# A transformer layer on one core: the attention groups written out in halves after a table of places, zero rows filled by transfers, four chunks projected in front, and the tail taken apart

## The reference

```python
x = x + attn(layernorm(x))            # x: 2 x 1024 x 128, f32; 16 heads of width 8
x = x + moe(layernorm(x))             # 2048 tokens
# attn: q, k, v = x@W + b; rotary; att = (q@k.T + bias_of_distance[head]) / sqrt(8), causal,
#       softmax, @ v, then @ Wp + bp
# moe:  probs = softmax(x@Wr); top 2 of 8 experts; position of a token in its expert = running count;
#       512 places for each expert; expert: rms norm, gelu(h@Wg)*(h@Wu) @ Wd + row (128 -> 256 -> 128);
#       out = x + sum of weight*expert row; a token that found no place takes a small shared network (width 64)
```

## Time and profile before

| | us |
|---|---|
| median of 3 runs (lowest to highest) | 473.14 (470.46 to 474.53) |
| the profiled execution, whole | 469.73 |
| its span in the trace | 468.0 |
| PE busy | 383.5 |
| DVE busy | 320.2 |
| POOL busy | 277.1 |
| ACT busy | 212.4 |

### The profile page before, as it was taken

How to read it: one execution, slowest core, us unless ns; L and a number is a source line. 1 busy time by engine, 2 the same in 40 slices (tenths; PEclk the granted TensorE clock), 3 DMA queues, 4 the chain that set the end, 5 groups by cost and what they waited for, 6 DMA issues and landing times.

```text
span 468.0 us, 8283 instructions
## 1 busy us (share of the span) xinstructions
PE 383.5 (82%) x2440; PEld 184.4 (39%) x2440; DVE 320.2 (68%) x702; ACT 212.4 (45%) x471; POOL 277.1 (59%) x229
## 2 busy tenths in 40 slices
PE   3497398699999999997999999985976494999910
PEld 0154143343444434433444444342434151566510
DVE  3989379687786786865867868759566770366614
ACT  1024212377676776764767767755442100233200
POOL 6637800096767857865768668575457383066760
PEclk9999679799999999999999999998897597899975
DMA  7296880650532883507107100062001011123118
GB/s 232 36 275 136 180 191 15 167 97 2 101 74 92 261 183 68 111 5 125 50 4 134 39 4 1 1 201 70 2 30 56 26 45 63 48 91 92 46 45 269
DMA packets 32560, 42.90 MB, mean 92 GB/s; under 512 B 6043, under 2 KB 26395, under 8 KB 31147
## 3 DMA queue, kind: packets, MB, share of 16 engines
q1 hardware_dynamic: 29334, 35.62, 32.5%
q0 software_dynamic: 2048, 4.11, 2.6%
q10 hardware_dynamic: 1136, 2.65, 1.6%
HBM read 27.61 MB, written 12.75 MB: 86 GB/s over the span
## 4 chain that ended last, share of the span: by engine, by line
PE 63%; DVE 15%; DMA 7%; issue 6%; POOL 5%; SPq 1%; ACT 1%; ACTq 0%; DVEq 0%; POOLq 0%
PE ps_av L923 15%; PE ps_st L899 14%; PE ps_slot L827 13%; PE ps_slot L831 5%; PE ps_st L1018 3%; PE ps_slot L1028 3%; POOL slots L609 3%; DVE neg_max L1182 2%; DMA b_grp<-b_all 2%; PE ps_st L1020 2%; PE ps_slot L942 1%; PE ps_av L1020 1%; DMA bcol<-in_L_attn_bk_dram 1%; PE ps_slot L866 1%; POOL parts L618 1%
## 5 line engine op out<-in xcount | busy, mean ns | idle before, releaser
L1182 DVE TENSOR_REDUCE neg_max<-ps_slot 128x1 f32<-128x640 f32 (+7 forms) x184 | 175.9, 990 | 46.4 <-PE ps_slot L831 45.2
L689 ACT ACTIVATE probs<-ps_st 128x512 f32<-128x512 f32 (+3 forms) x384 | 164.6, 494 | 86.4 <-PE ps_st L899 83.5
L594 POOL TENSOR_TENSOR probs<-probs,f_grp 128x960 f32<-128x960 f32 (+2 forms) x70 | 133.8, 1916 | 5.2
L827 PE MATMUL ps_slot<-k_stack,q_stack 128*128 128x512 bf16 (+3 forms) x384 | 102.7, 335 | 9.4 <-DMA b_grp<-b_all 3.4
L899 PE MATMUL ps_st<-q_stack,k_stack 128*128 128x512 bf16 (+3 forms) x384 | 99.8, 332 | 4.3 <-DMA q_stack<-max_rows 2.7
L590 POOL TENSOR_SCALAR_AFFINE_SELECT probs<-probs 128x512 f32<-128x512 f32 x63 | 40.2, 638 | 102.3 <-ACT probs L689 102.3
L923 PE MATMUL ps_av<-probs,v_grp 128*32 128x512 f32 (+3 forms) x768 | 82.3, 502 | 0.6 <-POOL probs L594 0.3
L831 PE MATMUL ps_slot<-b_grp,flip_b 128*128 128x240 bf16 (+2 forms) x288 | 67.6, 259 | 0.0
L899 PEld LDWEIGHTS ps_st<-q_stack,k_stack 128*128 128x128 bf16 x384 | 34.8, 98 | 65.8 <-ACT probs L689 45.8
L827 PEld LDWEIGHTS ps_slot<-k_stack,q_stack 128*128 128x128 bf16 x384 | 36.3, 100 | 47.4 <-DVE neg_max L1182 14.5
L618 POOL DMA_INDIRECT parts<-probs,e_tok x32 | 31.5, 985 | 31.0 <-DVE probs L1434 22.2
(11 more groups left out here) (156 smaller groups left out, 392.2 us busy)
## 6 DMA issues: line engine op xcount, KB each, us to landing
q_stack<-q_parts SPq DMA_DIRECT2D x24, 192.0 KB
f_grp<-f_all SPq DMA_DIRECT2D x6, 512.0 KB, 10.2
slots<-in_c_rows_dram SPq DMA_DIRECT2D x4, 528.0 KB, 6.1
probs<-slots SPq DMA_DIRECT2D x8, 264.0 KB, 2.7
f_all<-g_vec SPq DMA_DIRECT2D x1, 2048.0 KB, 11.3
k_stack<-k_parts SPq DMA_DIRECT2D x16, 128.0 KB
b_grp<-b_all SPq DMA_DIRECT2D x8, 256.0 KB
...
```

What stands on the lines that cost most here:

```text
L594: pool.tensor_tensor(pr, pr, f_grp[:, fbuf, :, fo:fo + hi - lo], ALU.mult).then_inc(near_done, 1)
L689: act.activation(probs[:, u % PBUF, g, c0:512], ps_st[:, n % 3, c0:512], ACT.Exp, scale=SCALE).then_inc(exp_done, 1)
L827: pe.matmul(ps_slot[:, slot, o + lo:o + hi], q_stack[:, buf, g, t * P:(t + 1) * P], k_stack[:, buf, g, lo:hi], start=True, stop=(nlo >= nhi))
L1182: dve.tensor_reduce(neg_max[:, heads[0]:heads[-1] + 1, t], src, AX.X, ALU.max, negate=True).then_inc(slot_used, 1)
```

## The change

The loop is gone: `attention_plan` builds one list (`PLAN`) for the whole of prologue, attention and tokens, and every engine walks it. Eight groups of 48 rows (one ST each) are numbered 0 to 383, and `S_BEFORE`, `M_BEFORE`, `EXTRAS` and `DISPATCH_AT` say ahead of which row or behind which unit each piece stands.

- q and k stacks are stored and loaded by halves of 512 tokens. Group 0's halves go out and in first; its S starts with the first half; M comes twice for each group (`NM` = 2), and ST of query half 0 waits for the first alone.
- S of group 0 stands partly ahead of row 0 (13 units) and partly within its own ST; S of group 1 at rows 16 to 50, later groups about one group ahead.
- No memsets: rows 72 to 79 (8 partitions) and 80 to 127 (48 partitions) are filled by transfers out of a row of zeros (`clear_rows`, on ACT's queue: buffer 0 at the start, buffers 1 and 2 in `LOAD`; and a first one on SP's). `LOAD`, also on ACT, brings the bias tiles of the twelve later heads. The small weights are loaded from POOL's queue.
- `v_all` holds values at a pitch of 9 with the column of ones; AV reads 9 columns from it, and the zero padding and the copy on ACT go. `f_grp` and `b_grp` go too: bias tiles are read from `f_all` and `b_all`.
- All 16 tiles are normed in one go on DVE; chunks 1 to 3 are normalised on ACT. All four chunks are projected in front; the split and the storing of chunks 2 and 3 stand within group 0's ST, and so do six of eight FLIP.
- Batch 0's tokens are worked in groups 3 to 5, with its Newton steps on POOL and its rows on ACT, and its 16 dispatches on POOL in groups 6 and 7. Batch 1 is two spans of four tiles: the first is dispatched while the last is being worked. A and C go through `ps_st` and ACT. F and G stand behind everything, and the scaling of their weights with them.
- Warm-up matmuls are 128 columns wide: 48 and 24 in front, 10 and 6 in the tail, 8 before the experts (before: 8, 8 and 32 of 512 columns).

```diff
-VW = 32
+MAX_ROWS, CLEAR = 3, 80
+VW = D + 1
-STACK_IN = 10 * 16
-PART_OUT = 4 * 16
+STACK_IN = 9 * 16
+HALF_IN = 8 * 16
+NM = 2
+MT = TPB // NM
+PART_OUT, REST_OUT = 8 * 16, 6 * 16
-WARM_FIRST, WARM_STACK, WARM_SLOTS = 8, 8, 32
+WARM_FIRST, WARM_PROJ, WARM_SLOTS = 48, 24, 8
...
+M_AT = (6, 22)
+S_BEFORE = [
+    [0, 0, 0, 0, 0, 0, 0, 0, 0, 0, 0, 0, 0, 2, 4, 5, 6, 7, 7, 10, 11, 12, 13],
+    [16, 16, 16, 16, 16, 17, 18, 20, 23, 24, 24, 27, 28, 28, 31, 35, 35, 36, 38, 41, 43, 47, 50],
+    [52, 56, 56, 58, 59, 63, 66, 68, 72, 72, 75, 76, 76, 79, 79, 82, 82, 84, 86, 89, 91, 95, 98],
...
+M_BEFORE = [(0, 16), (21, 54), (71, 102), (119, 150), (167, 198), (214, 245), (262, 300), (310, 342)]
+DISPATCH_AT = [73, 75, 77, 79, 81, 83, 84, 85, 86, 87, 88, 89, 90, 91, 92, 93]
...
-SPANS = [(0, TPB), (TPB, TT)]
+SPANS = [(0, TPB), (TPB, TPB + CH), (TPB + CH, TT)]
+LAST_NEAR = [2, 3, 5, 7, 9, 10, 11]
...
+LAST = [("DISP", j // 2, j % 2) for j in range(len(DISPATCH_AT), 2 * TPB)] \
+    + [("C", 2), ("AV", NG - 1, NU - 3), ("RI", 1), ("D", 1), ("AV", NG - 1, NU - 2)] + choose(1) \
+    + [("AV", NG - 1, NU - 1), ("EVAC", NG - 1, 1), ("Y", NG - 1, 1), ("PR", 1)] + place(1) \
+    + [("A", 3), ("B", 3), ("WARM", 10), ("BN", 3, 0), ("BN", 3, 1)] + [("RS", 2, j) for j in range(4)] \
+    + [("U", t) for t in range(TT - CH, TT)] + [("RI", 2), ("C", 3), ("D", 2), ("WARM", 6)] + choose(2) + [("PR", 2)] + place(2)
...
+        def clear_rows(eng, first, n, done):
+            for st, rows in ((q_stack, (M_ROW, CLEAR)), (q_stack, (CLEAR, P)), (k_stack, (CLEAR, P))):
+                eng.dma_start(st[rows[0]:rows[1], first:first + n, :, :, :].rearrange("p a h b c -> p (a h b c)").bitcast(F32),
+                              bass.AP(tensor=c_ones.tensor, offset=MAX_ROWS * NBUF * HG * T // 2,
+                                      ap=[[0, rows[1] - rows[0]], [1, n * HG * T // 2]])).then_inc(done, 16)
...
+            for c in range(2):
+                store_part(c, 0, (0,), first_out[0])
+                store_part(c, 1, (0,), first_out[1])
+                sp.wait_ge(first_out[0], 16 * (c + 1))
+                load_q(0, 0, (c,), half_in[c])
+                sp.wait_ge(first_out[1], 16 * (c + 1))
+                load_k(0, 0, (c,), half_in[c])
+            store_parts(0, (1, 2, 3), parts_out[0])
+            store_parts(1, (1, 2, 3), parts_out[1])
+            put_max(0, 0)
+            for c in range(2):
+                sp.wait_ge(parts_out[c], REST_OUT)
+            sp.wait_ge(zero_in[1], 48)
+            load_stack(1)
+            put_max(0, 1)
+            load_stack(2)
+            for n in range(1, NG):
+                put_max(n, 0)
...
+                elif kind == "LOAD":
+                    act.wait_ge(vec_out, 32)
+                    act.wait_ge(half_in[1], HALF_IN)
+                    load_tiles(act, b_all, r_vec, HG, H - HG, toep_rest)
+                    load_tiles(act, f_all, g_vec, HG, H - HG, factors_rest)
+                    clear_rows(act, 1, 2, zero_in[1])
...
+                    if g == 0 and (qb, kt) in ((0, 0), (1, 0)):
+                        pe.wait_ge(mrows_in[qb], 16 * MAX_PARTS * (n + 1))
...
                     for g in range(HG):
-                            mm = pe.matmul(ps_av[32 * g:32 * g + VW, c0:512], v_grp[:, vb, kt, g, :],
+                        mm = pe.matmul(ps_av[32 * g:32 * g + VW, c0:512], v_all[:, n, kt, g, :],
...
+                    elif su == 0:
+                        pe.wait_ge(stack_in[n % NBUF], STACK_IN * fill_of(n))
+                        if n == 1:
+                            pe.wait_ge(zero_in[1], 48)
+                            pe.wait_ge(toep_rest, 16)
...
+            def first_roots(piece):
+                v, t, dst = newton[:, 0:2, 0:TPB], newton[:, 2:4, 0:TPB], rstd[:, :, 0:TPB]
+                if piece == 1:
+                    pool.wait_ge(guess_done, 1)
+                after(pool.tensor_tensor(t, dst, dst, ALU.mult))
+                after(pool.tensor_tensor(t, t, v, ALU.mult))
+                after(pool.tensor_scalar(t, t, -0.5, 1.5, ALU.mult, ALU.add))
+                after(pool.tensor_tensor(dst, dst, t, ALU.mult))
```

More of the change, by code:

```diff
@@ new lines, in score_items @@
+def score_items():
+    out, late = [], []
+    for n in range(NG):
+        for su in range(len(SUNITS)):
+            out.append((S_BEFORE[n][su], ("S", n, su)))
+            late = [(left - 1, m) for left, m in late]
+            if su in M_AT:
+                late.append((M_LATE if n else 0, ("M", n, M_AT.index(su))))
+            while late and late[0][0] <= 0:
+                m = late.pop(0)[1]
+                out.append((M_BEFORE[m[1]][m[2]], m))
+    return out + [(M_BEFORE[m[1]][m[2]], m) for _, m in late]
@@ L483, in _, with stack_rows @@
[L483 to L492 removed]
+            load_tiles(sp, b_all, r_vec, 0, HG, toep_in)
+            load_tiles(sp, f_all, g_vec, 0, HG, factors_in)
+            def stack_rows(stack, buf, row, n, halves):
+                return stack[row:row + n, buf, halves[0]:halves[-1] + 1, :, :].rearrange("p h g t -> p h (g t)")
@@ L976, in _ @@
+            for what in FALLBACK:
                 kind, c = what
```

1396 lines of the change are left out of this document (743 added, 653 removed), and 13 rows, old and new, of tables (EXTRAS, S_BEFORE).

## The result

The changed kernel takes 479.0 us (median of 4 runs, 477.6 to 480.7), the kernel before 472.7 in the same comparison: ratio 1.0137, 95% interval 1.008 to 1.019. It is slower by a little over 1%, clear of noise, where the forecast was 434 and faster. The profiled execution has a span of 476.5. The page's totals say little: PE is busy for 10 us more than before, and the low stretches of its clock, in slices 6 to 8 and behind the attention, are still there, at other places.

The account below looks back on a forecast made before the run. PE was taken to bound the loop's steps, leaving gains around them. Stages of 43 + 58.5 + 191.4 + 26 + 41.5 + 70.6 gave a 431.0 us span, 432.7 whole, forecast 434; range 422 to 451.

Parts of the forecast that it names:

- Vectors, turn and the first projection are as before: Front: these pieces keep their earlier times, so the first rotation starts near 19.5 us instead of 27.3.
- The pace of the chunks: Front: a chunk costs DVE 5.4 us, four chunks 22; then two FLIP, and S starts at 43.
- 1.9 to land, more under load: First S to group 1: landing time of the first half's maxima rows, putting them in q at 53 to 55 us.
- Rival 1: Zeroing and LOAD are late, put_max(0,1) queues behind load_stack(1), row 16 starts at 82 to 84: +11, 445 us; chance 0.17.
- The rate I took, 260 GB/s: First S to group 1: rate seen in the trace, held against rival 1's front mean of 172 GB/s for 5.1 MB.
- Six steps of 30.5 are 183.2: Groups 1 to 6: base time at the old loop's step, before token work, savings and waits bring it to 191.4.
- AV's saving: Groups 1 to 6: nine instead of 32 columns take 0.02 us off each of 96 units, 2 in all.
- rival 4: AV's nine-column matmuls are not run side by side: +225 us, about 650, so slower; chance 0.04.
- Rival 2: The middle groups stretch: each of seven groups takes 3 us more than forecast, 453 us; chance 0.12.
- The distance over 33: Groups: the forecast fails if like points lie over 33 us apart; 30.5 to 32 was expected for groups 1 to 6.
- ST of group 7: Last ST group: ACT's 23.5 us bounds it, most token units gone; 26 us instead of 36.5, gain 10.5.
- Tail: Last exponential to first expert matmul: last places at 23, F and G wholly behind, fold at 41.5; gain 12.9 us.

Follow-up runs that it names:

- e1: Changed kernel with 10 and 4 warm-up matmuls in front instead of 48 and 24: 469.8 us, ratio 0.9927 to the kernel before.
- e9: Changed kernel with short front warm-up, weights early on ACT's queue, LOAD behind the last turn, output bias in four later pieces, S and ST over 75 rows: 462.1 us.
- e12: e9 with the tail's warm-up matmuls 512 columns wide, and two such matmuls behind each of group 0's 13 early S units: 454.4 us, ratio 0.9610.
- e3: Changed kernel with POOL's output bias addition moved from the prologue to unit 13: 478.8 us, ratio 1.0126 to the kernel before.
- e2: Changed kernel with LOAD's five transfers issued by SP behind its own tile loads instead of by ACT: 468.3 us, ratio 0.9878 to the kernel before.
- e10: Changed kernel with batch 0's token units moved back into group 7 and its 16 dispatches behind that: 489.5 us, ratio 1.036 to the kernel before.
- e5: Changed kernel with the rows of S for groups 2 to 7 put back to the earlier kernel's cadence, M at rows 10 and 44: 489.0 us, ratio 1.036.
- e13: e12 with one pair of S units of groups 2 to 5 and 7 placed one row earlier: 453.7 us, ratio 0.957 to the kernel before.
- e14: e12 with each of the 16 turnings of the maxima (M) done twice into the same place: 456.4 us, ratio 0.964 to the kernel before.
- e11: Changed kernel with the tail's ten and six warm-up matmuls made 512 columns wide and written out: 480.1 us, ratio 1.014 to the kernel before.

## Why the prediction was wrong, step by step

- **To the first S, 43 forecast, 60.9 measured.** The step that failed is "Vectors, turn and the first projection are as before". The norm came as forecast (15.5, the four DVE normalises 1.1), but I priced the 72 narrow warm-up matmuls at nothing, when the list of the change names them: 9.2 us to the first rotation (e1). Of the 5.9 left between e1's 25.4 and the forecast's 19.5, 2.1 are a slip in my own sum. By its terms the first chunk is normed at 16 (e1: 15.9), and from the turn to the first rotation (21.68 and 27.27) the kernel before takes 5.6 us, which makes 21.6. The other 3.8 are ACT's: the weights land at 17.1 and its own list stands ahead of the turn's copy, so the first projection waits until 21.5. I had checked x alone, not the weights nor ACT. In e9 and e12, with the weights issued early, the first rotation comes at 23.5 and 23.3. Also unpriced: POOL's bias addition beside the rotation, 3.6 us (e3). The pace of the chunks held otherwise: first rotation to first S 22.9 in e9, forecast 23.5.
- **First S to group 1, 58.5 forecast, 68.9 measured.** From the first S to the first exponential I gave 11 (43 to 54) and it took 24.3; from there to row 16 17.5 and 17.5; from row 16 to group 1 30 and 27.1. The step that failed is the landing of put_max(0,0), "1.9 to land, more under load": 14.4. I had seen the burst of 5 MB and set it against put_max(0,1), 15 rows later; LOAD stood ahead of both. Rival 1 had the mechanism and named the wrong place; it was worth 11 us (e2), which was its price. The rate I took, 260 GB/s, holds for the bias tiles; the zero rows moved at 134.
- **Groups 1 to 6, 191.4 forecast, 202.2 measured.** Tokens were put at 6.7 of PE and part of 3 for waits, and cost 10.0 (e10). The step that failed is "Six steps of 30.5 are 183.2": a group without tokens takes 31.85, six times 1.3 more, in waits for other engines, for which I gave 3 in all. Where they lie the rows show; what brings them about stays open (e5, e13, e14). AV's saving was right (0.24 a group measured, 2 in all forecast), and nine columns did stay side by side, so rival 4 is dead: a unit of 512 columns takes 0.97 to 0.98. Rival 2 foresaw the stretching, with 3 us in each group (its 453 should have been 455, 434 and seven times 3); it was 1.8 on average. The distance over 33 that I had named as a sign of failure came in groups 3 to 6, 33.4 to 35.7.
- **ST of group 7, 26 forecast, 27.3 measured.** Right in mechanism and size.
- **Tail, 41.5 forecast, 47.5 measured.** F to the fold took 18.3 as forecast (18.5) and DVE's fold released the experts, not the slots' load, as forecast. Mis-sized is the time to the last places, 23 forecast, 28.7 measured: the attention's last projection was added at 13.8 instead of 10, and the router's logits came 9.8 behind it instead of 7. Both lie at the low clock, which I had read for F alone. By the rows, A 3, B 3, C 3 and D 2 pay about 2.9 us for it together, half of the 5.7 (an estimate, from twice their time at the full clock); no run shows it, since e11 brought the clock back for C 3 and part of D 2 alone, and what makes the other half is open.
- **What hid the loss.** Gains of 8.6 in the last ST and 7.0 in the tail were real and were eaten by 15 us in groups 1 to 6 and 10 ahead of them, against before.
